# One run of 64 receivers' rows and one 512-column one-hot product for groups 0 to 79 of a graph network's first layer

## The reference

```
# layer 1: an MLP over edges, gated, averaged by source node
h = concat([x[src], x[dst]])              # 50000 x 512
h = tanh(h @ W0 + b0)                     # 406 wide
h = tanh(h @ W1 + b1)                     # 323 wide
h = (h @ W2 + b2) * (edge_attr @ Wg)      # 256 wide
x = layernorm(x + segment_mean(h, src))
# layer 2: attention with four heads over the same edges, softmax by dst
x = layernorm(x + attention(x, src, dst))
```

## Time and profile before

| | |
|---|---|
| median of 3 runs | 2240.55 us (2239.36 to 2241.13) |
| span of the profiled execution | 2239.4 us |
| TensorE busy | 1938.9 us, 87% |
| VectorE, ScalarE, GpSimd busy | 68%, 62%, 66% |
| bytes moved | 370.78 MB, mean 166 GB/s |
| loads into TW | 196 of 203 KB |
| matmuls at L1536 | 784 |

### The profile page before, as it was taken

One profiled execution on the slowest core, in us unless ns is written; L12 is line 12 of the kernel. 1 busy time (PEld: TensorE's weight loads), 2 busy tenths in 40 slices (PEclk: granted clock), 3 DMA queues, 4 the chain that ended last, 5 costly groups with the idle time before them and its releaser, 6 DMA issues.

```text
span 2239.4 us, 40504 instructions
## 1 busy us (share of the span) xinstructions
PE 1938.9 (87%) x12932; PEld 1717.4 (77%) x12932; DVE 1513.0 (68%) x3765; ACT 1377.2 (62%) x2758; POOL 1488.4 (66%) x1229
## 2 busy tenths in 40 slices
PE   7799999999999999999999999999664676666660
PEld 6699999999999999999999999999653455445450
DVE  6566676676666766766666667666565766666667
ACT  3488888888888888888888888888550000000012
POOL 0427677777777677777776767775427777777754
PEclk9899999999999999999999999999886767877785
DMA  7988877777777777776777777776555566656544
GB/s 241 297 221 188 201 167 171 165 161 172 158 168 171 149 167 159 154 167 152 159 165 149 166 159 154 167 153 129 119 183 142 148 160 158 161 154 162 155 125 128
DMA packets 233059, 370.78 MB, mean 166 GB/s; under 512 B 32743, under 2 KB 165825, under 8 KB 232839
## 3 DMA queue, kind: packets, MB, share of 16 engines
q0 software_dynamic: 101232, 188.20, 42.2%
q1 hardware_dynamic: 131607, 179.89, 27.5%
HBM read 270.57 MB, written 97.40 MB: 164 GB/s over the span
## 4 chain that ended last, share of the span: by engine, by line
PE 70%; POOL 14%; DMA 6%; issue 5%; DVE 4%; ACT 1%; SPq 0%; DVEq 0%; ACTq 0%; POOLq 0%
PE bank L1483 16%; PE bank L1482 16%; PE bank L1484 16%; POOL Hg L1407 13%; PE bank L1536 5%; PE bank L1527 5%; PE bank L1553 3%; DMA Hg<-HT,src_c 3%; PE bank L1577 2%; PE bank L1578 2%; PE bank L1589 2%; PE bank L1588 2%; DMA accA<-ystage,to_a 1%; PE bank L1654 1%; DVE xb L959 1%
## 5 line engine op out<-in xcount | busy, mean ns | idle before, releaser
L1369 POOL DMA_INDIRECT accA<-ystage,to_a x391 | 653.6, 1672 | 244.0 <-DMA accA<-ystage,to_a 113.9
L1375 POOL DMA_INDIRECT GA<-TA,src_c x391 | 424.9, 1087 | 292.7 <-issue 95.4
L1407 POOL DMA_INDIRECT Hg<-HT,src_c x391 | 378.3, 968 | 121.1 <-issue 112.8
L1482 PE MATMUL bank<-h1h,W1h 128*128 128x512 f32 x882 | 348.4, 395 | 0.0
L1484 PE MATMUL bank<-h1h,W1l 128*128 128x512 f32 x882 | 347.5, 394 | 0.0
L1483 PE MATMUL bank<-h1l,W1h 128*128 128x512 f32 x882 | 347.5, 394 | 0.0
L563 DVE TENSOR_TENSOR h2l<-h2f,h2h 128x512 fp32r<-128x512 f32 (+1 forms) x294 | 203.1, 691 | 200.8 <-ACT h2l L1769 130.5
L1698 PE MATMUL bank<-xb,in_window 128*128 128x260 f32 (+1 forms) x782 | 273.1, 509 | 58.6 <-issue 56.9
L1944 ACT ACTIVATE drop<-neg_m 128x1 f32<-128x1 f32 x49 | 14.4, 295 | 455.0 <-DVE neg_m L954 455.0
L563 DVE TENSOR_TENSOR h1l<-h1f,h1h 128x512 fp32r<-128x512 f32 x294 | 195.1, 691 | 129.5 <-ACT h1h L1769 129.5
L1698 PEld LDWEIGHTS bank<-xb,in_window 128*128 128x128 f32 (+1 forms) x782 | 190.4, 256 | 103.9 <-issue 68.4
(11 more groups left out here) (217 smaller groups left out, 4819.2 us busy)
## 6 DMA issues: line engine op xcount, KB each, us to landing
TW<-TB SPq DMA_DIRECT2D x196, 203.0 KB, 3.5
ef<-in_eT SPq DMA_DIRECT2D x97, 256.0 KB, 4.6
bcast_i<-in_src_row SPq DMA_DIRECT2D x97, 256.0 KB, 5.6
HB<-hist SPq DMA_DIRECT2D x98, 130.0 KB, 3.1
rel<-RL SPq DMA_DIRECT2D x97, 128.0 KB, 5.6
rem<-RD SPq DMA_DIRECT2D x48, 256.0 KB, 4.6
TB<-stB SPq DMA_DIRECT2D x24, 406.0 KB, 4.5
accA<-zeros SPq DMA_DIRECT2D x4, 1677.0 KB, 13.7
```

Of the source, the lines that this page charges most:

```text
L1369: return pool.indirect_dma_start(out=table, out_offset=bass.IndirectOffsetOnAxis(ap=rows, axis=0), in_=sums, in_offset=None, compute_op=AL ...
L1375: pool.indirect_dma_start(out=GA[0:n, b % (GAR * BLOCKS_PER_GROUP), :].bitcast(f32), out_offset=None, in_=TA, in_offset=bass.IndirectOffse ...
L1407: pool.indirect_dma_start(out=Hg[0:n, slot, :], out_offset=None, in_=HT, in_offset=bass.IndirectOffsetOnAxis(ap=src_c[0:n, b:b + 1], axis= ...
L1482: pe.matmul(o, lh, rh, start=first, stop=False)
```

## The change

For groups 0 to 79 `runs_of_group` gives a single run of all 512 edges; later groups keep two halves. The single window starts at the group's lowest receiver: VectorE adds N = 3125 to `ends[:, 0]` for groups from 80 on and takes the minimum of that and the halves' starts, so both halves of an early group get the group's start. SyncE issues as many loads as there are runs, TensorE multiplies each run, and the wait for s_tw counts loads.

```diff
+WHOLE_RUNS = 80
+    def runs_of_group(g):
+        return [(0, GE)] if g < WHOLE_RUNS else [(0, HE), (HE, GE)]
+        run_end = sb("run_end", [NG, 1], f32, sn)
                 const(dve.tensor_tensor(ends[:, k:k + 1], halves[:, 0:1], halves[:, 1:2], op))
+            const(dve.tensor_scalar(run_end[:, :], p_f[0:NG, :], float(WHOLE_RUNS), float(N), ALU.is_ge, ALU.mult))
+            const(dve.tensor_tensor(run_end[:, :], run_end[:, :], ends[:, 0:1], ALU.add))
+            const(dve.tensor_scalar(ends[:, 2:4], ends[:, 2:4], run_end[:, :], None, ALU.min))
             const(dve.tensor_tensor(high[:, :], high[:, :], ends[:, 2:4], ALU.subtract))
...
-                for i in range(2):
+                for i in range(len(runs_of_group(g))):
                     first = sp.value_load(low2_i[0:1, i, g:g + 1], min_val=0, max_val=2 * (N - 1))
...
-                    pe.wait_ge(s_tw[g % TWR], 32 * (g // TWR + 1))
+                    pe.wait_ge(s_tw[g % TWR], 16 * sum(len(runs_of_group(i)) for i in range(g % TWR, g + 1, TWR)))
...
-                for i in range(2):
-                    v = slice(i * HE, min((i + 1) * HE, e))
+                runs = runs_of_group(g)
+                for i, (a, z) in enumerate(runs):
+                    v = slice(a, min(z, e))
                     last = pe.matmul(PT[u % 2][0:k1(c), v], TW[:, g % TWR, i, c * P:c * P + k1(c)],
-                                     hot1[:, g % TWR, v], start=False, stop=i == 1)
+                                     hot1[:, g % TWR, v], start=False, stop=i == len(runs) - 1)
```

## The result

The changed kernel took 2237.77 us (median of 15 runs) beside 2241.41 us of the kernel before (15 runs of the same session): a ratio of 0.9983, 95% interval 0.9977 to 0.9990, which is 3.6 us less (2.2 to 5.2 by the interval). In a second comparison on fresh runs it took 2238.81 us (11 runs) beside 2241.14 us (33 runs), ratio 0.9990, 0.9981 to 0.9999, 2.3 us less (0.2 to 4.3 by the interval). The forecast was 2238.3 us and 2.3 us less.

What follows compares the result with a forecast made beforehand. TensorE was taken to bound the layer's middle, transfers and clock its ends. Products -1.7, start loads -1.1 and VectorE operations +0.5 gave -2.3 us: 2238.3 us from a median of 2240.55, range 2234.3 to 2242.6, verdict "same".

Steps and rivals of the forecast that it cites:

- TensorE bounds the layer; loads in its middle are worth nothing: Layer's middle: TensorE busy 300.00 of 300 us, so its savings count; 16.6 MB less load traffic gains nothing.
- Two products of 256 for one of 512: TensorE, groups 0 to 79: 320 fewer matmuls, about 0.005 us saved per chunk, -1.7 us (0 to -3.2).
- The exposed weight load stays: TensorE, product after the transposes: the 0.07 us stall belongs to the first weight load; 0.30 us expected where 0.31 stood.
- rival 2: TensorE: the exposed 0.07 us stall goes with the second product, 17 us more, -19.3 in all, 2221.2 us; chance 0.04.
- Three operations: VectorE ahead of L618: threshold, sum and minimum delay TensorE's restart, +0.5 us (0.3 to 0.6 at unchanged clock).
- Rival 3: TensorE's first wait: longer idling prolongs the half-clock stretch, 3.4 us more, +2.3 in all, 2242.9 us; chance 0.08.
- The start: Layer's start: two fewer window loads (groups 0 and 1) among the stores of TB, -1.1 us (0 to -3.2).
- rival 1: Layer's start: SyncE's 1.9 us and 1.3 us of traffic both count, -4.6 us in all, 2235.9 us; chance 0.14.
- The sum: Whole kernel: products -1.7, start -1.1, three operations +0.5, together -2.3 us; chance of this case 0.70.
- The signs: Profile after: period 15.42 us for 15.44, L1510 near 23.1 us, TensorE's first continuous work near 91.9 instead of 92.72.
- First work before 90.5 us: Layer's start: TensorE's first continuous work this early would make the prediction wrong and point to rival 1.
- 0.50 beyond 28.6 us: First half-clock stretch: granted clock staying at 0.50 past 28.6 us would make the prediction wrong and point to rival 3.

Runs made afterwards that it cites:

- the products alone: Kernel before with one 512-column product per chunk in groups 0 to 79 and the three VectorE operations, still two TW loads per group: 2406.89 us beside 2405.59, ratio 1.0005.
- the loads alone: Kernel before with one TW load per group and the three VectorE operations, still two 256-column products per chunk: 2404.61 us beside 2405.59, ratio 0.9996.
- 96 groups: Changed kernel with the threshold at 96 instead of 80, so 16 more groups with one window and product: 2237.70 us beside 2241.14 of the kernel before, ratio 0.9981.

## Why the prediction was right, and where its sizes were off

- *TensorE bounds the layer; loads in its middle are worth nothing.* Shown: the pace changes with the products alone.
- *Two products of 256 for one of 512: -1.7 us.* Measured -1.2. The single product's own distance fell as forecast: summed over the 312 chunks of 78 groups, start to next start, from 90.92 to 89.30 us, 5.3 ns for each of the 308 changed ones. But the transposes' sum rose from 87.39 to 87.66 us, and smaller shifts at other lines make up the rest. The forecast took those neighbours as unchanged; their reaction is the 0.5 us. Why they react stays open: the transposes' sum is 87.64 us with the products alone and 87.63 with the loads alone.
- *The exposed weight load stays.* Shown: 0.30 us for one product. The one row of before in which a lone product paid the same 0.07 us decided the largest question of the case, 17 us, and rival 2 is out. With it falls, in this case, the reading of the Trainium skill's sentence (TensorE: Matmul & The Clock Gate, Architectural detail: the array is 16× 32×32, not 1× 128×128), that a matmul can begin before its weight load completes: whatever begins early here, its product is not done sooner. That page's rule for a weight load, columns / 1.2 in ns (LDWEIGHTS (loading the stationary operand)), gives an estimate of 107 ns for 128 columns; the 0.11 us between the two weight loads of the earlier trace rows agree.
- *Three operations: +0.5 us.* Measured 0.65 on VectorE's way (7.68 for 7.03), steady over all profiles. Nothing behind it takes the delay back: from TensorE's restart to the last L1482 product of the node tables it is 54.49 and 54.37 us in the two profiles of before, 54.54 and 54.83 in those of the changed kernel. In whole times it was not seen. The clock did not answer: of the profiles with the three operations none kept the first half-clock stretch beyond 29.6 us, and none had it longer than 6.9 us. Rival 3 did not come.
- *The start: -1.1 us.* Measured -1.8 (-2.1 and -2.3 within the two chips that have both kinds). This was a term with wide ends (0 to -3.2); the measured value lies between the forecast and rival 1's -3.2. That the second window loads of groups 0 and 1 hold up the work behind the stores of TB is shown: the start follows these two loads, whatever the products are. How they do it is not. The -1.1 counted bytes alone; whether SyncE's time makes up the missing 0.7 us the runs cannot say, for neither moving bytes out of the way (0.1 us) nor sending the stores out sooner (0.3 us) gave a gain that one can tell.
- *The sum.* -1.2 + 0.65 - 1.8 = -2.35 us beside -3.6 and -2.3 measured, and -2.3 predicted. The start erred by 0.7 us one way, the products and the operations by 0.5 and 0.15 the other, so that the sum came out this close by luck. The range, 2234.3 to 2242.6 us, holds no change at all as well; the whole time alone could not have told this mechanism from none. The 1.2 us by which the first comparison is larger is within its interval and has no cause that I could show.
- *The signs.* First work at 90.67 us rather than 91.9, the period at 15.425 us for 15.42, L1519 (L1510 before) at 22.74 and 22.49 us for 23.1. "First work before 90.5 us" did not occur; it was close. "0.50 beyond 28.6 us" did occur by the letter, at 28.9 and 29.5 us, but as a shift: the stretch began later and was not longer, so the sign was drawn too sharply for what it was to show.

None of the versions tried is clearly faster than the changed kernel. With 96 groups 0.3 us more are gained in the layer, at the price of a threshold that, by the estimate above, these data barely allow.

## What to carry to other kernels

Count what a merged matmul saves from start to start, and look whether the stall in front of it belongs to the one that goes or to the one that stays: an odd-sized case somewhere in the trace often shows a lone product with the same neighbour. Behind a bound engine, 80 loads were worth nothing, and the two of them that stood between critical stores were worth at least as much as 320 matmuls (1.8 and 1.2 us). A gain of 0.1% is read from distances between fixed points of the profile, which repeat to hundredths in a steady loop, and not from whole times. Outside the loop they don't: the start differs by a microsecond between two profiles of the kernel before, so that a gain of that size there takes several profiles of either kind.

## What the runs showed of the hardware

The pace of 78 groups repeats to 0.07 us in 1204 us, across chips as well (1204.35 to 1204.42 us with two products and two loads, 1203.13 to 1203.17 with one product). The kernel before takes 2241 us on one chip and 2399 to 2406 us on two others, and most of that lies in the second layer: from the last product with W1s to the end 641.8 us in one profile and 793.9 in the other. Most of the rest is the longer way to group 2 described above. The engines' work is the same, as the page of the slower profile shows beside the earlier trace rows:

```profile
PE 1952.6 (81%) x12932; PEld 1728.3 (72%) x12932; DVE 1513.5 (63%) x3765; ACT 1377.4 (57%) x2758; POOL 1484.5 (62%) x1229
```

What differs is VectorE's wait at the scores, which read gathered rows: first the faster chip, then the slower (us in total, times, longest; for the slower one the view names no transfer, only a remote releaser):

```profile
DVE score L921 <- DMA Hg<-HT,src_c: 137.9, 40, 5.8
```

```profile
DVE score L921 <- remote: 285.4, 37, 30.7
```

That it is the gathered rows that come later there is inferred from what the line reads; why they would was not looked into.
